# Two of nine query fills issued from ScalarE's queue, and the third normalisation placed one step later, in a one-core decoder block

## The reference

```python
x = x + self_attention(layernorm(x), Wq, Wk, Wv, Wo)            # 16 heads of 8, causal, rotary
x = x + cross_attention(layernorm(x), ctx, W_kv, W_q, W_proj, b_proj)   # 16 heads of 8
h = layernorm(x)                                               # the third normalisation
probs = softmax(h.mean(axis=1) @ gate_w)                       # one routing for a whole sequence
top_w, top_i = top_k(probs, 2); top_w = top_w / top_w.sum()
x = x + sum(top_w[k] * (gelu(h @ w1[e] + b1[e]) @ w2[e] + b2[e]) for k, e in enumerate(top_i))
```

## Time and profile before

| | value |
|---|---|
| median of 3 runs | 182.52 us (182.29 to 182.76) |
| profiled execution, its own time | 183.2 us |
| its span, first to last instruction | 181.4 us |
| mean granted TensorE clock | 0.981 |
| PE busy | 163.8 us, 90% of the span |
| DVE busy | 130.1 us, 72% |
| ACT busy | 104.5 us, 58% |
| POOL busy | 67.6 us, 37% |
| DMA moved | 18.39 MB, 101 GB/s on the mean |

### The profile page before, as it was taken

The page is one execution under the profiler, slowest core; times in us unless marked ns, Lnnn a source line. Parts: engine busy times, 40 slices in busy tenths (PEclk is TensorE's granted clock), DMA queues, the critical chain, the costliest instruction groups (busy, mean ns, idle before and its releaser), DMA issues.

```text
span 181.4 us, 4454 instructions
## 1 busy us (share of the span) xinstructions
PE 163.8 (90%) x1536; PEld 119.2 (66%) x1536; DVE 130.1 (72%) x500; ACT 104.5 (58%) x218; POOL 67.6 (37%) x132
## 2 busy tenths in 40 slices
PE   5779996979999899599899989989999998989994
PEld 4458775756767566467667656756666465879983
DVE  4488499698798889688988988999965454642120
ACT  2055622157675666465667867778746765972351
POOL 6836929278911560241232223201261071124310
PEclk9988997999999999999999999999999999999999
DMA  5914264167176165154044145103503501705401
GB/s 155 291 21 127 69 154 131 45 155 194 19 184 174 34 137 130 44 141 108 18 123 115 29 105 125 40 4 101 166 7 90 171 0 30 234 29 171 125 29 29
DMA packets 23449, 18.39 MB, mean 101 GB/s; under 512 B 2428, under 2 KB 21372, under 8 KB 22780
## 3 DMA queue, kind: packets, MB, share of 16 engines
q1 hardware_dynamic: 22672, 17.20, 35.5%
q10 hardware_dynamic: 756, 0.92, 2.0%
HBM read 12.08 MB, written 2.29 MB: 79 GB/s over the span
## 4 chain that ended last, share of the span: by engine, by line
PE 61%; DVE 21%; issue 5%; POOL 4%; DMA 4%; SPq 2%; ACT 2%; POOLq 0%; DVEq 0%; ACTq 0%
PE psV L985 11%; PE psB L963 9%; PE psA L939 8%; DVE negmax L673 8%; PE psA L1029 6%; PE psV L1046 4%; PE psB L876 4%; DVE masked L667 3%; PE psM L853 3%; DVE xn L626 3%; PE psA L1046 2%; PE psA L922 2%; DMA stackQ<-hid 2%; PE psB L968 2%; SPq L397 2%
## 5 line engine op out<-in xcount | busy, mean ns | idle before, releaser
L807 ACT ACTIVATE E<-psB 128x512 f32<-128x512 f32 x112 | 62.2, 595 | 26.3 <-PE psB L968 16.0
L939 PE MATMUL psA<-stackK,stackQ 72*128 72x256 bf16 (+1 forms) x256 | 41.6, 261 | 6.1 <-DVE negmax L673 2.1
L673 DVE TENSOR_REDUCE negmax<-psA 128x2 f32<-128x512 f32 x64 | 40.6, 680 | 4.4 <-PE psA L939 4.2
L963 PE MATMUL psB<-stackQ,stackK 74*128 74x256 bf16 (+1 forms) x256 | 41.3, 259 | 0.6
L667 DVE CUSTOM_DVE_ANT_0 masked<-psA,row_mask 128x128 bf16<-128x128 f32 (+1 forms) x128 | 36.8, 347 | 6.0 <-PE psA L939 6.0
L939 PEld LDWEIGHTS psA<-stackK,stackQ 72*128 72x128 bf16 x256 | 21.7, 98 | 16.4 <-DVE negmax L673 4.6
L985 PE MATMUL psV<-E,V 128*18 128x256 f32 (+1 forms) x512 | 30.5, 356 | 0.0
L963 PEld LDWEIGHTS psB<-stackQ,stackK 74*128 74x128 bf16 x256 | 21.8, 97 | 7.4 <-ACT E L807 3.1
L523 POOL TENSOR_SCALAR rstd<-mv 128x2 f32<-128x2 f32 x12 | 2.7, 227 | 56.0 <-DVE mv L621 56.0
L985 PEld LDWEIGHTS psV<-E,V 128*18 128x18 f32 x512 | 11.9, 97 | 13.0 <-issue 6.5
L968 PE MATMUL psB<-mask16T,ident 128*128 128x256 bf16 (+1 forms) x48 | 14.8, 309 | 0.0
(11 more groups left out here) (112 smaller groups left out, 249.3 us busy)
## 6 DMA issues: line engine op xcount, KB each, us to landing
stackK<-scratch SPq DMA_DIRECT2D x18, 192.0 KB
stackQ<-hid SPq DMA_DIRECT2D x36, 64.0 KB
w1s<-w_dram SPq DMA_DIRECT2D x8, 258.0 KB, 2.8
w2s<-w_dram SPq DMA_DIRECT2D x8, 256.0 KB, 4.1
stackQ<-scratch SPq DMA_DIRECT2D x2, 576.0 KB
stackK<-hid SPq DMA_DIRECT2D x16, 64.0 KB
scratch<-parts_ctx SPq DMA_DIRECT2D x12, 64.0 KB
stackQ<-scratch ACTq DMA_DIRECT2D x1, 576.0 KB
```

What stands on the lines that cost most here:

```text
L673: dve.tensor_reduce(negmax[:, b, heads[0]:heads[-1] + 1:2, t], scores, AX_X, ALU.max, negate=True).then_inc(a_taken, 1)
L807: act.activation(dst, psB[:, bank].rearrange("p (h q) -> p h q", h=dst.shape[1]), ACT.Exp, scale=SCALE).then_inc(b_taken, 1)
L939: last = pe.matmul(psA[:, bank, i * keys:(i + 1) * keys], stackQ[0:ROWS, b, h, t * P:(t + 1) * P], stackK[0:ROWS, b, h, 0:keys], start=Tru ...
L963: last = pe.matmul(psB[:, bank, i * n:(i + 1) * n], stackK[:, b, h, t * P:(t + 1) * P], stackQ[:, b, h, q0:S], start=(s == 1 or i == 0), s ...
```

## The change

It has two parts. First, of the nine fills of the cross queries, the two with i = 2 and r = 1, 2 are taken from SP's list and issued by ACT, at a new step `stack_help` three halves later (m + 8). Second, for the cross jobs of b = 0, 1, 2 `ln_apply` of the third normalisation moves from the end of half m + 3 into half m + 4, behind the first two units of it; `ln_turn` moves from the middle to the end of half m + 5; and `route_mean`, `route`, `route_pick` and `route_weights` move one half later. For b = 3 nothing of this moves.

```diff
@@ plan() @@
         put(m + 2, "ln_stats", s + 1, b)
-        put(m + 3, "ln_apply", s + 1, b)
-        if (s, b) == (1, NB - 1):
+        if s == 0:
+            put(m + 3, "ln_apply", s + 1, b)
+            between.setdefault(m + 5, []).append(("ln_turn", s + 1, b))
+        elif b == NB - 1:
+            put(m + 3, "ln_apply", s + 1, b)
             put(m + 4, "ln_turn", s + 1, b)
         else:
-            between.setdefault(m + 5, []).append(("ln_turn", s + 1, b))
+            between.setdefault(m + 4, []).append(("ln_apply", s + 1, b))
+            put(m + 5, "ln_turn", s + 1, b)
         if s == 0:
             put(n + 24, "stack_read_k", 1, b)
             put(m + 5, "q_cross", 1, b)
             put(m + 5, "stack_fill", 1, b)
+            put(m + 8, "stack_help", 1, b)
         else:
-            put(m + 5, "route_mean", 2, b)
-            put(m + 6, "route", 2, b)
-            put(m + 7, "route_pick", 2, b)
-            put(m + (9 if b < NB - 1 else 7), "route_weights", 2, b)
+            late = 1 if b < NB - 1 else 0
+            put(m + 5 + late, "route_mean", 2, b)
+            put(m + 6 + late, "route", 2, b)
+            put(m + 7 + late, "route_pick", 2, b)
+            put(m + 7 + 3 * late, "route_weights", 2, b)
@@ SP @@
                 if kind == "stack_fill" and s == 1:
                     for i in range(NPART):
-                        for r in range(NPART):
+                        for r in range(NPART if i < NPART - 1 else 1):
                             fill_q(b, i, r, parts_q[b])
@@ ACT @@
+                if kind == "stack_help":
+                    i = NPART - 1
+                    act.wait_ge(parts_q[b], NPART)
+                    for r in range(1, NPART):
+                        act.dma_start(stackQ[i * BLOCK + r:(i + 1) * BLOCK:NPART, b], parts[:, b, 0, i]).then_inc(q_in[b], 16)
```

## The result

The changed kernel takes 183.91 us (median of 22 runs) beside 182.78 us of the kernel before on the same chips (22 runs): ratio 1.0076, 95% interval 1.0050 to 1.0103. By that ratio it is slower by about 1.4 us, where the prediction had +0.34 us and gave the largest chance to a change that can't be told from none. The time lies 0.01 us above the upper end of the range, which was 183.9. All ratios here are taken over the fast runs of both kernels and can differ by up to 0.4% from the quotient of the two medians.

What follows compares the result with a forecast made beforehand. Bounds taken: late fills at 72 to 76 us, DVE at the last cross boundary, PE's waits in the tail. Terms 0 + 0.1 + 0.44 - 0.2 = +0.34 us on the median 182.52 gave 182.9 us, range 181.8 to 183.9.

Steps and rivals of the forecast that it cites:

- the second place: Boundary between the last two cross jobs, 115 to 132 us: DVE waits only 0.2 us and sets the time.
- the first place: Start of the cross jobs, 72 to 76 us: the last fill of b = 0 is late; up to 0.96 us winnable.
- The 1.58 us of the earlier trace: PE's standstill for the fills of b = 0 before the first cross maxima at 74.11 us.
- landing of the fills: Part one's term for fills landing sooner: 0 us, between a gain of 0.96 and a loss of 0.3 us.
- the prediction's own list: Signs in the profile after: PE's fill wait over 1 us, DVE's near 1.0; below 0.3 the first step is wrong.
- The backlog sum: Fills move from 67.5 us at about 0.53 us each; nine end at 72.3 on the mean, slowest share 74.1.
- Fills that were queued earlier wait longer: Claim in the fills' term that earlier issue brings no earlier landing; the term is 0 us.
- ACT's side: Two issues in ACT's queue for each b, 1.95 us a pair, delay what follows on ACT: +0.1 us for all four.
- The second rival: ACT's help delays the attention output: 1.4 us instead of 0.1, so 184.2 us; chance 0.17.
- Part two, b = 0: Last cross boundary: the moved normalisation leaves DVE waiting 0.49 us for the turned maxima; +0.44 us, between 0.2 and 0.6.
- Part two, b = 1 and b = 2: b = 1: 0 us; b = 2, tail: values start earlier unless ACT's exponentials hold them, -0.2 us (0 to -0.36).
- the bound of what can be told: A measurement tells about 0.3% (0.55 us) from no change; the forecast of +0.34 us lies inside that.

Runs made afterwards that it cites:

- first_undone: The changed kernel with part two undone for b = 0 alone, against the kernel before: 183.02 against 182.59 us, ratio 1.0012.
- norm_alone: The kernel before with part two of the change and nothing else: 184.10 against 182.26 us, ratio 1.0066.
- route_late: The kernel before with only the four routing steps of b = 0 to 2 one half later: 183.17 us, ratio 1.0061.
- after: The changed kernel in its first profile, at 184.96 us; measured 183.91 against 182.78 us of the kernel before, ratio 1.0076.
- rows_second: The kernel before with max_rows behind the first maxima unit of the next job at every boundary: 180.05 against 182.40 us, ratio 0.9874.
- fills_alone: The kernel before with part one of the change and nothing else: 182.55 against 182.26 us, ratio 1.0017.

## Why the prediction was wrong

**What bounds the kernel now.** The reading of the second place was right: DVE sets the time from 115 us to u0, and what it loses there comes out at u0 (13.89 to 14.84, back to 13.89 in `first_undone`). The reading of the first place was wrong. The 1.58 us of the earlier trace rows, and the 1.2 us that they cost, belonged to one execution. The prediction named this as where it fails most easily, but gave it a chance of 0.20 and took the number all the same.

**Part one, landing of the fills.** "0 us" was right for the wrong reason. The fills landed at 71.67 instead of 74.06 us, PE's wait for them is gone and DVE took up the turned maxima at 74.60; by the prediction's own list this makes the step wrong. But kernels without ACT's help show nearly the same (`norm_alone`, `route_late`). The backlog sum had given a mean end of 72.3 us, within the 72.0 to 72.9 of the four ordinary profiles without help: that held, and its last clause, that the slowest share lands at 74.1, was the accident. What the help does bring, some 0.7 us of the 1.3 us of issue, half contradicts "Fills that were queued earlier wait longer", and it is worth nothing because next to nothing waits. The Trainium skill, "DMA: Bandwidth & Descriptors", section "Issuing engines are not separate DMA queues", says that issuing from several engines saves only the sequencer's time. The trace agrees in so far as the fills became shorter by less than the 1.3 us of issue; the ratio of 1.0017 does not contradict it and, being no change clear of noise, does not test it. The eight engines of a fill, from the same page's rule on the largest number of engines that divides both sides, agree with the share of 0.52 in the stretch from 67.5 to 70.6 us; it is a little above one half, and no view here shows which engines carried a fill.

**Part one, ACT's side.** +0.1 us was forecast, 0 measured: the four pairs of after take 1.27 to 1.37 us instead of 1.95 and start under or together with the exponential ahead. For b = 2 they hold the next exponentials for 0.44 us, but the idle 0.65 us ahead of `oNT` take that up, as the pair is 0.7 us shorter than the sum had it: c5 to c6 and c6 to c7 have not moved (13.91 and 14.48 to 14.50). The second rival, with +1.4 us from this cause, gave nearly the measured time, 184.2 us, and none of it came from there. A time that fits is no evidence for its mechanism.

**Part one, SP's side.** The sum had no term for it. Of SP's queue only the issues taken away were counted, and not that everything behind them shifts, the row maxima of c4 among it. The piece c4 to c5 costs 0, 0.20, 0.49, 0.66 and 1.20 us with the help (five profiles, the third on `rows_second`), 0.51 on the mean; in the five kernels of the table without it, it varied by 0.01 us. The wait behind c3 comes on top, in kernels with and without help. Part one alone measured +0.3 us, with an interval of 0.5 us to either side, so that this part costs anything at all is not shown by the times.

**Part two, b = 0.** This is the step that failed: +0.44 us predicted (0.2 to 0.6), +0.95 us measured, in three profiles to 0.01 us. The mechanism that was named is right: the uncovered wait for the turned maxima came as worked out (0.49 predicted, 0.48 seen). What the step left out, as if it cost nothing, is the routing product. Its move was followed for SP's loads and for b = 2, but for b = 0 not for DVE: `route` waits for a product that now stands behind 1.06 us of values, 0.44 us. `route_late` shows that this half of part two costs 0.67 us by itself. The normalisation adds 0.27 us to that, within the range of its term; what it costs with the routing in its old place no run shows.

**Part two, b = 1 and b = 2.** b = 1 cost nothing, as said. For b = 2 -0.2 us were taken and none came: 49.56 us before, 49.54 after. The routing product did leave its place ahead of the values, but ACT now waits 0.51 us for the turned `xn`, its exponentials are later by what PE had won, and the values wait 0.23 us for them. The reservation "unless ACT's exponentials hold them" was the case.

**The sum.** Predicted 0 + 0.1 + 0.44 - 0.2 = +0.34. Measured piece by piece: 0 for ACT, 0.95 for b = 0, 0 for b = 2, and some 0.3 us for part one as a whole: +1.25, against 1.39 us (interval 0.9 to 1.9) for the change. The forecast stood only 0.2 us below the bound of what can be told, and two of its terms erred to the same side by 0.5 and 0.2 us; the missing one for SP's side, worth some 0.3 us if anything, points the same way.

## What to carry to other kernels

When a step is moved, ask for each of its instructions on each engine what stands directly ahead of it there in the new place, and who stands still meanwhile; a small product behind a long one costs its consumer the long one's time if that engine is the bound. Before building on one late transfer, look whether its siblings in the same trace are late too: one of four sets of fills was waited for here, and in that execution it lasted 9.6 us where eight others without help had 7.6 to 8.2. Where two engines hand work to and fro at a boundary, the cheap gain is to give the bound engine a unit it already has data for while the other turns the old result: that one move, with no work removed, brought 1.3%. And when the moved step is itself the mark of a ruler, measure from a step that stays.

## What the runs showed of the hardware

- Reads of instructions go through the same 16 DMA engines as the data: twelve of 16 KB (q8) and nine of 8 KB (q14) in the profile of after. Taking issues out of SP's queue went with one of the 8 KB reads at 76.9 to 78.2 us instead of 72.8 to 75.3, right behind a pair of SP's issues that then took 1.57 to 1.97 us instead of 1.20. The coincidence is shown, the mechanism is not.
- An issuing pair of this shape took 1.27 to 1.37 us on ACT in the profile of after, beside running exponentials, and 1.52 us once in `fills_alone`; at the start of the kernel, beside SP's issues, it took 1.95 us. The exponential behind it began 0.1 us after the pair's end each time: issuing runs beside the instruction ahead, and holds the one behind.
- The same two copies of row maxima (8 KB each, c3) made PE wait 0 to 0.48 us in five profiles without help and 0.76 to 1.00 us in four with it, though nothing ahead of them in the program differed.
- Single times of the kernel before went from 181.0 to 186.4 us over the 22 runs of the comparison, where the three runs given first spanned 0.5 us. With 12 to 22 runs the intervals were still 0.25 to 0.4% to either side, wider than the +0.34 us that the forecast was about.
